# Loads reordered, a busy TensorE at the start, first and last steps of an attention and expert kernel moved between engines

## The reference

```python
xn = _layernorm(x, axis=-1)
x = x + _L0_attn_ref(xn, wq, wk, wv, wo) + _L0_ffn_ref(xn, router_w, w1, w2, w3)
# attention: 16 query heads, 4 key/value heads of 16 numbers, rotary positions, causal softmax
q, k = apply_rope(q, cos, sin), apply_rope(k, cos, sin)
attn = softmax(where(mask, -inf, q @ k.T / sqrt(16)));  out = (attn @ v) @ wo
# experts: 8 of 64 hidden numbers, the two best of each token, bfloat16 inputs
h = silu(x1) * x3;  routed = h @ w2;  weighted = routed * scores
```

## Time and profile before

| | us |
|---|---|
| runs | 290.53, 290.76, 291.65; median 290.76 |
| profiled execution, its own time | 290.62 |
| its span | 288.9 |
| busy: TensorE, VectorE, ScalarE, GpSimd | 262.5, 227.5, 244.4, 125.8 |
| mean granted clock of TensorE | 0.994 |

### The profile page before, as it was taken

How to read it: one execution, slowest core, us unless ns; L and a number is a source line. 1 busy time by engine, 2 the same in 40 slices (tenths; PEclk the granted TensorE clock), 3 DMA queues, 4 the chain that set the end, 5 groups by cost and what they waited for, 6 DMA issues and landing times.

```text
span 288.9 us, 6905 instructions
## 1 busy us (share of the span) xinstructions
PE 262.5 (91%) x2307; PEld 115.8 (40%) x2307; DVE 227.5 (79%) x312; ACT 244.4 (85%) x518; POOL 125.8 (44%) x260
## 2 busy tenths in 40 slices
PE   0868599999999999999999998999999999999996
PEld 0534355434344233334343443445523233433454
DVE  3663978999999999998999999995799898033342
ACT  1589876988999999999999998986689989898941
POOL 8386657363458418951135335246005414035020
PEclk9999889999999999999999999999999999999999
DMA  7537074110307103407371001023000300131307
GB/s 238 168 74 138 14 125 110 40 20 2 75 1 111 23 0 77 109 15 120 86 172 41 2 3 37 3 57 73 1 3 16 97 3 0 41 72 19 75 18 166
DMA packets 49106, 17.67 MB, mean 61 GB/s; under 512 B 43120, under 2 KB 48560, under 8 KB 49072
## 3 DMA queue, kind: packets, MB, share of 16 engines
q1 hardware_dynamic: 48384, 16.43, 26.8%
q10 hardware_dynamic: 688, 0.79, 0.8%
HBM read 4.46 MB, written 2.10 MB: 23 GB/s over the span
## 4 chain that ended last, share of the span: by engine, by line
PE 64%; DVE 12%; issue 8%; ACT 6%; POOL 5%; DMA 4%; POOLq 0%; SPq 0%; ACTq 0%
PE ps L808 18%; PE ps L790 13%; DVE PM L657 11%; PE ps L775 10%; PE ps L749 6%; PE ps L827 4%; ACT PR L543 3%; PE ps L848 3%; DMA HT<-HB 3%; PE ps L817 2%; PE ps L767 2%; PE ps L846 2%; PE ps L739 2%; DMA STACKS<-MIXED 1%; PE ps L835 1%
## 5 line engine op out<-in xcount | busy, mean ns | idle before, releaser
L543 ACT ACTIVATE PR<-ps,SCALE 128x512 f32<-128x512 f32 (+1 forms) x320 | 182.5, 654 | 15.7 <-PE ps L790 13.5
L657 DVE TENSOR_REDUCE PM<-ps 128x8 f32<-128x1024 f32 x144 | 167.8, 1218 | 9.0 <-PE ps L775 7.7
L453 POOL TENSOR_SCALAR_AFFINE_SELECT PR<-PR 128x512 f32<-128x512 f32 x64 | 39.8, 635 | 94.7 <-ACT PR L543 94.7
L808 PE MATMUL ps<-PR,VA 128*32 128x512 f32 (+3 forms) x768 | 78.1, 495 | 0.5 <-ACT OA L550 0.5
L790 PE MATMUL ps<-STACKS 64*128 64x512 f16 (+3 forms) x384 | 75.2, 327 | 2.9 <-ACT PR L543 1.4
L775 PE MATMUL ps<-STACKS 64*128 64x128 f16 (+2 forms) x640 | 59.2, 263 | 5.4 <-DVE PM L657 3.7
L790 PEld LDWEIGHTS ps<-STACKS 64*128 64x128 f16 x384 | 24.3, 93 | 57.0 <-ACT PR L543 43.6
L775 PEld LDWEIGHTS ps<-STACKS 64*128 64x128 f16 x640 | 27.1, 95 | 36.7 <-issue 32.1
L468 POOL TENSOR_TENSOR HB<-MIXED,GATE 128x512 bf16<-128x512 f32 x16 | 16.5, 1043 | 30.0 <-DVE MIXED L711 29.6
L808 PEld LDWEIGHTS ps<-PR,VA 128*32 128x32 f32 x768 | 17.0, 108 | 25.9 <-issue 21.1
L749 PE MATMUL ps<-WP,XT 128*128 128x392 f32 x64 | 25.7, 536 | 1.6 <-ACT XT L489 1.6
(11 more groups left out here) (92 smaller groups left out, 234.0 us busy)
## 6 DMA issues: line engine op xcount, KB each, us to landing
X<-x SPq DMA_DIRECT2D x8, 256.0 KB, 6.3
out<-X SPq DMA_DIRECT2D x16, 128.0 KB, 1.9
MIXED<-w SPq DMA_DIRECT2D x3, 512.0 KB, 3.8
STACKS<-MT SPq DMA_DIRECT2D x64, 2.0 KB
WP<-w_proj ACTq DMA_DIRECT2D x1, 392.0 KB, 4.3
WO<-wo ACTq DMA_DIRECT2D x1, 256.0 KB, 6.2
STACKS<-MIXED SPq DMA_TRANSPOSE x16, 3.6
MT<-MPW SPq DMA_TRANSPOSE x16, 2.5
```

What stands on the lines that cost most here:

```text
L453: mask = g.affine_select(out=blk, in_=blk, compare_op=ALU.is_ge, fill=0.0, base=0, pattern=[[0, GRP], [1, P]], channel_multiplier=-1)
L543: a.activation(PR[:, k % RING, j, 0:width], bank(step)[:, 0:width], ACT.Exp, scale=SCALE[:]).then_inc(s_exp, 1)
L657: v_.tensor_reduce(spots, two_banks(step).rearrange("p h (a s n) -> p h a s n", a=2, n=P), AX.X, ALU.max).then_inc(m_max, 1)
L808: mm = t_.matmul(o_bank[VW * j:VW * (j + 1), CHUNK - width:CHUNK], VA[:, b * KVH + grp, kb, :], PR[:, n % RING, j, at:at + width], start=i ...
```

## The change

Loads: SP issues two loads of x, waits for w_proj, and issues the other six; wo moves from ScalarE's queue behind them. TensorE does nine transposes of IDF before its list. GpSimd's frames become a step F of its list, behind the first two n; MPW's memset is among them. VectorE gets steps i (the sum) and l (the low parts) of tiles 0 to 3, and GpSimd keeps those of tiles 4 and on. For tiles 8 to 15 GpSimd also makes the high parts, and waits itself for the DMA transpose of the tile two before. The output becomes Y (with HT and W2) and y (with AT and WO), each placed on its own in TensorE's list. HELD goes from 4 to 6, and SP's hidden step waits for Y. All five strings of ORDER are new; TensorE's stand here whole, the start and end of the others.

```diff
+FIRST_LOADS = 2
+WARMING = 9
...
-HELD = 4
+HELD = 6
+AHEAD = 4
...
 ORDER = dict(
     PE=(
-        "xpxxPjjjxxxjxxjjjjmmmmmxxxmmJmJmmJmxmxxmJmJxmmJmsxmJmssmssmssmssmsvssmssmvssmsvmssmJmsmssvsmsssmvmss"
-        "smvsmssmvsmssssmssmsvsmsmssvrrsssrsmvssmsmvsmssvmssmssmssvmsssmvsmssmvssmssmsvmsssmvsmssmsvssmsmssms"
-        "vmsssmvsssmvmssmssmsvsmssmsvmsssmvmssrrssmsvssmsssvsssvmsssvsmssrsvssmmssvssmmssvssmsvmsssmsmsvmsssm"
-        "vssmsssmssmsvmssvmsmssvssmmssvssmsmsvssmsmvsmssvmssrsrsssmsmsvmssvmssmvssessEssvvssrrmssmssmvsssmmss"
-        "seessmvvEaamsssmvmssseEseymsssmvssmvssmaEEssyssrerssyvssmmssvaaeEssyymssvmssmsvmsssmvssmmssvmsssmvms"
-        "ssmvssmsseessEEessvmssmvssvmssEEssevmassmvsrsmssmsvsmssymsssmvssmssmsssvssvavsssyaasessvssyssEEssvss"
-        "vssyasseessvssEEssvsaevsssyssyssrrssvssvssveavEEryaaayayyy"),
+        "xpxPxjjxxjjxxjjxjjmmmmmxxmJmxxmJmJmmJxmxmJmssmssmssmssmJmsxmvsmsssmssmsvxmssmvssmJmssmsvmsssmJmssmvm"
+        "sssmsvmssmsvmsssmssmvssmvrrsssrmsmssvmsssmvmsssmvsmsssmvssmmsssvmssmsvsmssmsvmsssmvsmssmsvmssmssmssm"
+        "vsssmvsmsmssvssmmssvmssvmsssmvsmssmssmsmsssmvssmsrrssmvmsssmvmsssmvsmssmssvsmssvsmssvssvsssvsrssmssm"
+        "ssmssmvssmmssvmsssmvsmssmvssmsvmsmssvsmssmsvmssmssmsvsssmmssvssmvssmsrsrsseessEvssevssvEEssrrssmsvsm"
+        "sssmssmsvsmsvmsssmvssammsssvmssveessaeYYyymassEYssEEessyvssmmssvssmvsmssrrasmssmvssmsvmsmssvssmsmsvm"
+        "ssamvsssmsEssevsseemssvEvssmYYssyssymsssmvsmssvsmesrssEEssmvssmasmvsssmvmssmvssYYssyaeaayssvEsseYssy"
+        "EssvssvssvssYessEYsysssvssesvasvssyssreEssvssvssEEssYavvYarryyaaYYyyaaYYyy"),
     ACT=(
-        "xNxNxzzjllxxNNzzljjlxxNxjjNjNjjNllzzzxxzzxllJzzJJxxxJJlzxJlsxJssssssssssssssssssvJssssssssssvsssssss"
...
-        "ssvassssesessssassesssssssssssevaaaaa"),
+        "xxNNzzjlxljNxNxzlxljzjxxNjjNNjjNllzzxxzzJzzxlzxlzJJJxxJsssssssssJxsssssssxssssvJsssssssJsssssvssssss"
...
+        "sssssseasssssessssssssvaaaaaa"),
     DVE=(
-        "nnzWzzpnPjjznjjjjjjmmmmmMmmmmmmmMmmmmMmmmmmMmmmmmmmmmmmmmMmmmmmmmrrbbrbmmmmmmmMmmmmmmmmmmmmmMmmmmmmm"
...
-        "mmmmmmmmmeMEEeemmmEEemmrbmmmymmmmMyyEeEyeeEEyeyrrbbeEErbyyyyy"),
+        "nnzWzzpnPjijilzlnjijilljjjjmmmmmMmmmmmMmmmmmmmmMmmmMmmmmmmmmmmmmmMmmmmmmrrbbrbmmmmmmmmMmmmmmmmmmmmmm"
...
+        "mrrbbmmmmmmmmmMmEeemEemyymmmmrebEEmmmmmmMyeyyEEeyeeEyErbeEErrbbyyyyyy"),
     POOL=(
-        "nnnjjllnjjlljjRlljjMllqqMMlsssMqssssMsssssllqsssMlqssMslqqlqlssMslsMssMMMcccssssssMEsssssEEsEEMsssss"
...
-        "EMsEEEEsssMEEsssEEEE"),
+        "nnFnnjjRllMjjllMqqlssMMslsssqqsMssssssssMllqqsssMsllssMMqqllssMsccMsssscMMsssEEssEssssEssMEEsssMEEss"
...
+        "sEMEEsssEEEEE"),
     SP=(
-        "kkkkkktkkututtuutkukktutkukktkkuctcctuuttuuwtuwwyytwwuwtwwyyutuywwwwwwyyywwyyyyyyyy"),
+        "kkkkkktukktuttuutuktkkutkuktukkktcctcutuuttuuwwwtyyuwwtuwwyywtyyyuwwyywwywwwwyyyyyy"),
-FILLED_V = dict(project=1, maxima=2, untwisted=1, experts=1, factors=1, output=1)
+FILLED_V = dict(project=1, maxima=2, untwisted=1, experts=1, factors=1, share=1)
...
 PARTS = {
     ("ACT", "z"): range(CQ, TILES),
+    ("POOL", "j"): range(AHEAD, QT),
+    ("POOL", "l"): range(AHEAD, TILES),
     ("POOL", "s"): [(k + 1) * GRP - 1 for k, (_, i) in enumerate(PRODUCTS) if i < DIAGONAL],
     ("ACT", "v"): [k for k, product in enumerate(PRODUCTS) if ends(product)],
...
         @block.sync
         def _(sp):
             for n in range(LOADS):
+                if n == FIRST_LOADS:
+                    sp.wait_ge(w_in, 16)
                 sp.dma_start(X[:, 2 * n:2 * n + 2, :], x[2 * n * P:(2 * n + 2) * P, :].rearrange("(s p) d -> p s d", p=P)
                              ).then_inc(x_in[n], 16)
+            sp.dma_start(WO[:], wo.rearrange("(k p) n -> p k n", p=P)).then_inc(wo_in, 16)
             sp.wait_ge(ruled, 7)
             sp.dma_start(MASKS[ROWS:P], MASKS[0:ROWS]).then_inc(halved, 16)
...
                 elif kind == "hidden":
                     sp.wait_ge(gated, n + 1)
-                    after(sp, y_ps, n - HELD + 1)
+                    after(sp, y_half, n - HELD + 1)
                     sp.dma_start_transpose(HT[:, n % HELD], HB[:, n % 2]).then_inc(h_turned[n % 2], 16)
                 elif kind == "rows_placed":
                     b, c, grp = JOBS[n]
...
             g.memset(IDF[:], 0.0).then_inc(zeroed, 1)
             g.memset(MASKS[:], 0.0).then_inc(zeroed, 1)
-            g.memset(MPW[:], 0.0).then_inc(zeroed, 1)
             g.memset(NHALF[:], -0.5).then_inc(zeroed, 1)
-            pool.wait_ge(zeroed, 4)
+            pool.wait_ge(zeroed, 3)
             g.affine_select(out=IDF[:], in_=IDF[:], compare_op=ALU.not_equal, fill=1.0, base=0,
                             pattern=[[-1, P]], channel_multiplier=1).then_inc(made, 1)
             upper, last = slice(0, ROWS), ROWS - 2
...
                 g.affine_select(out=t[upper], in_=t[upper], compare_op=ALU.is_ge, fill=fill, base=last,
                                 pattern=[[0, t.shape[1]]], channel_multiplier=-1).then_inc(ruled, 1)
             g.memset(ONE[:], 1.0).then_inc(made, 1)
-            g.memset(TS[:, :, 0:QH, 3, :], 0.0).then_inc(framed, 1)
-            g.memset(TS[:, :, QH:SLABS, 3, 2:HD], 0.0).then_inc(framed, 1)
-            g.memset(TS[:, :, QH:SLABS, 3, 0:2], -1.0).then_inc(framed, 1)
-            g.memset(PM[:], -BIG).then_inc(framed, 1)
-            g.memset(VA[:, :, :, HD:VW], 1.0).then_inc(made, 1)
-            for e in range(E):
-                g.memset(RANK[:, e:e + 1], float(E - e)).then_inc(made, 1)
             for kind, n in steps_of("POOL"):
-                if kind == "moments":
+                if kind == "frames":
+                    g.memset(TS[:, :, 0:QH, 3, :], 0.0).then_inc(framed, 1)
+                    g.memset(TS[:, :, QH:SLABS, 3, 2:HD], 0.0).then_inc(framed, 1)
+                    g.memset(TS[:, :, QH:SLABS, 3, 0:2], -1.0).then_inc(framed, 1)
+                    g.memset(PM[:], -BIG).then_inc(framed, 1)
+                    g.memset(MPW[:], 0.0).then_inc(zeroed, 1)
+                    g.memset(VA[:, :, :, HD:VW], 1.0).then_inc(made, 1)
+                    for e in range(E):
+                        g.memset(RANK[:, e:e + 1], float(E - e)).then_inc(made, 1)
+                elif kind == "moments":
                     pool.wait_ge(ve, n + 1)
                     two = slice(2 * n, 2 * n + 2)
                     g.tensor_tensor(RSTD[:, two], VE[:, two], NHALF[:, two], ALU.pow).then_inc(rstd, 1)
...
                 elif kind == "project":
                     pool.wait_ge(rot, n + 1)
+                    if n == AHEAD:
+                        pool.wait_ge(roped, n)
                     after(pool, low, n - 1)
                     g.tensor_tensor(QK[:, n % 2], RC[:, n % 2], RR[:, n % 2], ALU.add).then_inc(roped, 1)
                 elif kind == "parts":
+                    heads = QK[:, n % 2].rearrange("p (h d) -> p h d", d=HD)
+                    if n >= QT:
+                        pool.wait_ge(turned_on, n - QT + 1)
+
+                        pool.wait_ge(stacked[n % 2], 16 * (n // 2))
+                        g.tensor_copy(TS[:, n % 2, 0:QH, 0:2, :], heads[:, 0:QH].unsqueeze(2).broadcast_to([P, QH, 2, HD]))
+                        twice = TS[:, n % 2, QH:SLABS].rearrange("p (g a) (b c) d -> p g (a b) c d", a=PILE, c=2)
+                        g.tensor_copy(twice[:, :, :, 0, :], heads[:, QH:HEADS].unsqueeze(2).broadcast_to([P, KVH, 2 * PILE, HD])
+                                      ).then_inc(high, 1)
+                    if n == AHEAD:
+                        pool.wait_ge(low, n)
                     pool.wait_ge(high, n + 1)
-                    heads = QK[:, n % 2].rearrange("p (h d) -> p h d", d=HD)
                     g.tensor_tensor(TS[:, n % 2, 0:QH, 2, :], heads[:, 0:QH], TS[:, n % 2, 0:QH, 0, :], ALU.subtract)
                     keys = TS[:, n % 2, QH:SLABS].rearrange("p (g a) b d -> p g a b d", a=PILE)
                     g.tensor_tensor(keys[:, :, :, 1, :], heads[:, QH:HEADS].unsqueeze(2).broadcast_to([P, KVH, PILE, HD]),
...
                            bank(step)[:, V_COL:R_COL].rearrange("p (g d) -> p g d", g=KVH)).then_inc(taken, 1)
                 elif kind == "parts":
-                    if n < QT:
-                        act.wait_ge(roped, n + 1)
-                    else:
-                        act.wait_ge(turned_on, n - QT + 1)
+                    act.wait_ge(roped, n + 1)
                     if n == 0:
                         act.wait_ge(framed, 3)
...
                     v_.tensor_tensor(rc, pj, cos, ALU.mult)
                     v_.tensor_tensor(rr[:, :, 0:half], pj[:, :, half:HD], sin[:, :, 0:half], ALU.mult)
                     v_.tensor_tensor(rr[:, :, half:HD], pj[:, :, 0:half], sin[:, :, half:HD], ALU.mult).then_inc(rot, 1)
+                elif kind == "sum":
+
+                    dve.wait_ge(rot, n + 1)
+                    after(dve, low, n - 1)
+                    v_.tensor_tensor(QK[:, n % 2], RC[:, n % 2], RR[:, n % 2], ALU.add).then_inc(roped, 1)
```

(31 more changed lines are left out.)

21 lines of the change are left out of this document (11 added, 10 removed).

## The result

The changed kernel takes 293.09 us (median of eight runs, 291.62 to 294.72), the kernel before 291.41 beside it. The ratio is 1.0066, with a 95% interval of 1.0037 to 1.0094: slower by two thirds of a per cent, where 288.7 us and "faster" had been forecast. One of the eight executions of the kernel before took 468.88 us; the ratio goes by the others, whose median is 291.28. The profiled execution took 294.72 us, its span is 292.9.

What follows compares the result with a forecast made beforehand. No single engine bounds the middle; TensorE bounds from 180 us on. Start -0.9, relief -1.6, split outputs +0.9 and tail -0.4 give -2.0 us: 288.7 us forecast, own range 287.3 to 289.8, whole range 285.6 to 291.0.

Steps and rivals of the forecast that it cites:

- the sum: Whole kernel: start -0.9, ScalarE's relief -1.6, split outputs +0.9 and tail -0.4 make -2.0 us.
- the start's term: Start up to the first maxima: they begin at 28.7 to 28.8 instead of 29.7; -0.9 us, 0 to -1.9.
- the relief of ScalarE: From 60 to 140 us: high parts of tiles 8 to 15 leave ScalarE (8.4 us); -1.6 us, 0 to -3.2.
- the transposes go at 17.4: Start: tile 3's normalisation done by 17.35 us, so its transposes go at 17.4.
- I take half: From 60 to 140 us: half of VectorE's 3.2 us idle time is won by relieving ScalarE, -1.6 us.
- GpSimd 13 more: GpSimd's busy time: high parts of eight tiles at 1.6 us each, 13 us more in all.
- The split outputs: Outputs in two steps, nearly all behind 180 us: TensorE changes its manner of working more often; +0.9 us, 0 to +1.4.
- 13 changes of manner: TensorE's switches between 64-row, 32-column and full-array work go from 249 to 262, at 0.11 us each, 1.4 us.
- The tail's wait for HT: End of the kernel: TensorE's wait for the last tile's hidden numbers goes; -0.4 us, 0 to -0.6.
- the nine transposes: Start, TensorE: added transposes don't raise the clock, 0 us; the rival with a high early clock (0.18) gave 287.7 or 286.5.
- The slower rival: GpSimd's in-order queue: masks wait behind new copies that wait for a transpose's landing; +3.6, 294.4 us; chance 0.10.
- Three quarters of 0.40: The forecast case (288.7 us, chance 0.40): its lower three quarters, given as 0.32, count as faster by over half a per cent.

Runs made afterwards that it cites:

- Two letters moved: Changed kernel with tile 9's stacking ahead of the sixth maxima's turning in SP's string, and their rows' placing ahead of tile 10's stacking: 1.0018, from 1.0066.
- tile 3 early: Tile 3's normalisation ahead of the sums and low parts in VectorE's string: 1.0047 in the changed kernel, 0.9986 in the kernel before with the changed start.
- the run meant for it: Changed kernel with the start of before (1.0048), tile 11's copies and parts behind one rotation and two masks in GpSimd's string: 1.0175.
- one letter here: Changed kernel with the start of before (1.0048), only tile 9's stacking moved ahead in SP's string: 0.9997.
- the one with u5 alone moved: Changed kernel with the start of before (1.0048), the sixth set's rows placed ahead of the stackings of tiles 9 and 10 in SP's string: 1.0134.
- the same with two letters moved: Kernel before with high parts of tiles 8 to 15 on GpSimd (1.0082), the steps for tiles 9 and 10 moved earlier in GpSimd's string: 1.0002.

## Why the prediction was wrong

Three steps failed: the sum has no term for the new order of SP's queue (1.4 us), the start's term has none for a further stretch of half clock (without one the start is 0.8 us ahead, with one 1.1 us behind), and the relief of ScalarE, -1.6, measured 0 on the order of before.

- **SP's queue, put at nothing.** The working follows GpSimd's and ScalarE's steps and says of SP only that its hidden steps can't be later. In the new order of its string k9, ready for 34 us, stands behind t5, and the rows behind k9 and k10. Two letters moved take the changed kernel from 1.0066 to 1.0018.
- **The start, -0.9 us.** The first step that failed in the trace is "the transposes go at 17.4" for tile 3: they went at 18.24, TensorE idle for 2.43 us before, and the two projections behind them ran at half clock. Tile 3's low parts ended at 26.4 for 24.7. The first projection was missed too (11.09 for 10.4): two normalisations beside memsets took 0.67 us more than before, where I had 0.25, and the first load came no sooner (4.63 for 4.66). With tile 3 early the maxima begin at 28.93, 29.01 and 28.45 in three kernels, near the forecast, but at 30.17 in the fourth; and their time is worth little. Between the kernel before with the changed start and the same with tile 3 early they move from 30.72 to 28.45, 2.3 us (one profile at 0.988, the other at 0.994), and the ratio by 0.0016, 0.5 us, less than the intervals can tell. As a whole the new start measured nothing on the old order (1.0002): 0.8 us gained in the executions at 0.994, 1.1 lost in those at 0.988. On the new order it measured 0.2% more time (1.0066 and 1.0048), which the intervals don't tell from none.
- **ScalarE's relief, -1.6 us.** On the order of before it measured 0 once the queues were free, so the step that failed is "I take half" of VectorE's idle time. In the new order it may hold: taken back at the places tried it costs 2.7 us. Why the old order has no use for it stays open. The copies cost 1.03 us a tile, not 1.6, and "GpSimd 13 more" left out the 7.9 us that move to VectorE.
- **The split outputs, +0.9.** In the new order of the rest, taking the split back costs 1.1%, 3.2 us, so its 13 changes of manner can't be seen against what the first steps fill. On another order it was not measured. The tail's wait for HT did go, but it was 0.3 us.
- **The clock.** Weighing the nine transposes at nothing was right (1.0059 without, 1.0066 with), and the first projections were slow as forecast, their weight loads 0.65 us apart. That a new idle gap can bring a half-clock stretch of its own was not in the sum. It is the failed part of the start's term.
- **The slower rival, 0.10.** It named GpSimd's queue in order, masks behind copies that wait for a landing, and gave 294.4 us. In part its kind is what ran, at less than its price: 4.7 us of waiting on GpSimd, once, and a wait of 1.1 us for rows beside it. The form that it described, a product waiting for a mask behind the copies, is what the kernel before with the high parts on GpSimd shows (1.40 us). What it missed is SP's queue: the landing was late because k9 stood behind t5, and the rows behind k9 and k10. It was set low because GpSimd waits 94.7 us for exponentials. That sum says nothing of a single place where two tiles and two rotations come in a row.
- **The chances.** Three quarters of 0.40 is 0.30, not 0.32. The range from 285.6 to 291.0 left out nearly all of the slower rival, which had 0.10.

What is left in the changed kernel after the two moves is 0.18%, within the interval of no change; that it lies in the start is argued, not shown. Whether GpSimd's wait or the rows' was the dearer in the changed kernel stays open: the run meant for it made a third one.

## What to carry to other kernels

When a change moves steps between engines whose queues run in order, list for each moved step what is queued behind it, on its own engine and on the one that issues its DMA, and give the latest time of the next thing a third engine needs; a wait that is short in sum or an engine with much slack in sum doesn't answer for a single place. A step that was ready long ago and is queued behind a late one is the first to move: one letter here was worth half a per cent. Price a part within the order it comes in: moving the same copies off ScalarE was worth nothing in one order, and moving them back cost up to 0.9% in the other. And sort the executions by their granted clock before a median is read: here that showed a gain and a loss in a part that measured zero.

## What the runs showed of the hardware

- Half clock came behind some single gaps of TensorE and not behind others. In the changed kernel it set in at 18.4 us behind 2.43 idle us, and in the kernel with the high parts on GpSimd at 93.5 behind 1.40; in the one with u5 alone moved a product waited 2.9 us at 112 and the clock stayed at 1.00, and so it did behind the 2.7 us of the kernel with tile 11's parts moved. The kernel with the high parts on GpSimd has 3.0 us more span than the same with two letters moved (291.8 and 288.8), of which the wait is 1.40; the rest fits the half clock behind it, 3.4 us at half speed, but was not measured apart.
- What one stretch of half clock goes with, in executions of one kernel at 0.988 and at 0.994: 291.97 and 290.06 us for the kernel before with the new start, 291.19 and 289.93 for the same with tile 3 early.
- Two VectorE normalisations took 1.40 us beside GpSimd's memsets (8.45) and 0.73 in the kernel before (8.75); the addition of epsilon took 1.06 us beside a memset and 0.17 without. The Trainium skill ("SBUF — State Buffer", on engine ports) says that VectorE's two-port modes and GpSimd exclude each other for a whole instruction; these rows agree with it.
- The same start does not start alike: in three executions with the start of before the first maxima began at 30.63, 29.41 and 30.77 us. A microsecond of difference there between two profiles is no finding.
